# Moving six steps of a scan out of the first norm's chain and into the first tiles of two fused transformer layers

## The reference, cut to what matters

```python
def step(H, inp):
    k_t, v_t, q_t, a_t = inp
    pred = jnp.einsum('bk,bkv->bv', q_t, H)
    err = jnp.sum((v_t - pred) ** 2, axis=-1, keepdims=True)
    surprise = jax.nn.sigmoid(err / (SURPRISE_TEMP + 1e-06))
    kH = jnp.einsum('bk,bkv->bv', k_t, H)
    delta = k_t[:, :, None] * (v_t - kH)[:, None, :]
    a = a_t[:, :, None]
    H = a * H + (1.0 - a) * (surprise[:, :, None] * delta)
    y_t = jnp.einsum('bk,bkv->bv', q_t, H)
    return (H, y_t)
...
x = x + ga * _L0_attn_ref(h, ...)
h = _layernorm(x, axis=-1) * (1 + cb) + sb
x = x + gb * _L0_ffn_ref(h, L0_ffn_w_gate_up, L0_ffn_w_proj)
```

## Time and profile before

| | |
|---|---|
| median of three executions | 1300.75 us |
| the profiled execution | 1301.84 us |
| its span, first to last instruction | 1299.9 us |
| mean granted TensorE clock | 0.880 |
| PE busy over the span | 1135.4 us (87%) |
| DVE busy over the span | 873.2 us (67%) |
| ACT busy over the span | 524.2 us (40%) |
| prefix and its start | 260.90 to 303.64 us |
| tiles 0 to 11 | 303.64 to 433.73 us |

### The profile page before, as it was taken

How to read it: one execution, slowest core, us unless ns; L and a number is a source line. 1 busy time by engine, 2 the same in 40 slices (tenths; PEclk the granted TensorE clock), 3 DMA queues, 4 the chain that set the end, 5 groups by cost and what they waited for, 6 DMA issues and landing times. The chain is left out here.

```text
span 1299.9 us, 13519 instructions
## 1 busy us (share of the span) xinstructions
PE 1135.4 (87%) x4632; PEld 602.2 (46%) x4632; DVE 873.2 (67%) x1602; ACT 524.2 (40%) x1091; POOL 169.7 (13%) x143
## 2 busy tenths in 40 slices
PE   5666879868999779989798988899998999989997
PEld 5423658645656334434344434344443444434443
DVE  3557775554666757879857886768887577883554
ACT  2433554324544236634326425236543163341421
POOL 3000000001111122211112112122301000110100
PEclk9667575556988889989899998999999999999999
DMA  7511111041222013323213001112120001100000
GB/s 219 176 33 33 43 39 49 1 162 49 83 81 81 1 48 113 116 58 111 71 50 95 24 25 57 41 33 87 40 65 9 1 21 63 47 32 1 1 33 32
DMA packets 47525, 75.57 MB, mean 58 GB/s; under 512 B 8321, under 2 KB 16001, under 8 KB 47329
## 3 DMA queue, kind: packets, MB, share of 16 engines
q1 hardware_dynamic: 47168, 74.62, 18.0%
q0 software_dynamic: 288, 0.09, 0.1%
HBM read 66.16 MB, written 8.54 MB: 57 GB/s over the span
## 5 line engine op out<-in xcount | busy, mean ns | idle before, releaser
L1560 PE MATMUL g_g<-h,wt 128*128 128x512 f16 x1728 | 410.6, 387 | 11.7 <-PEq L2440 6.7
L1560 PEld LDWEIGHTS g_g<-h,wt 128*128 128x128 bf16 (+1 forms) x1728 | 170.1, 99 | 236.0 <-issue 50.0
L1574 PE MATMUL g_d<-wt,parts 128*128 128x512 bf16 (+1 forms) x864 | 208.4, 383 | 7.9 <-DVE tmp L1672 3.5
L1483 PE MATMUL g_o<-shared 128*128 128x512 f32 x384 | 182.8, 620 | 16.3 <-ACT hf L2052 9.4
L2144 ACT ACTIVATE parts<-hid 128x512 f16<-128x512 f32 x108 | 68.1, 630 | 318.5 <-DVE hid L1842 313.0
L1835 DVE SCALAR_TENSOR_TENSOR hid<-th,g_g 128x512 f32<-128x512 f32 x108 | 73.6, 682 | 168.8 <-ACT th L2137 168.8
L1574 PEld LDWEIGHTS g_d<-wt,parts 128*128 128x128 f16 x864 | 84.0, 99 | 119.8 <-issue 23.0
L1483 PEld LDWEIGHTS g_o<-shared 128*128 128x128 f32 x384 | 75.2, 199 | 101.0 <-issue 73.9
L2251 POOL TENSOR_TENSOR acc<-acc,sqh 128x512 f32<-128x512 f32 x52 | 77.5, 1489 | 334.1 <-ACT sqh L2150 334.1
L1847 DVE TENSOR_TENSOR parts<-hid,parts 128x512 f16<-128x512 f32 x108 | 82.9, 768 | 31.9 <-ACT parts L2144 31.6
L1492 PE MATMUL g_o<-shared 128*128 128x512 f32 x128 | 64.2, 649 | 10.2 <-DVE shared L1919 5.2
(11 more groups left out here) (312 smaller groups left out, 1649.8 us busy)
## 6 DMA issues: line engine op xcount, KB each, us to landing
shared<-in_w SPq DMA_DIRECT2D x48, 256.0 KB, 2.7
x<-in_codes SPq DMA_DIRECT2D x32, 264.0 KB, 3.1
w_raw<-in_wt SPq DMA_DIRECT2D x16, 512.0 KB, 3.7
x<-in_wmod SPq DMA_DIRECT2D x7, 1024.0 KB, 5.2
wmod<-in_wmod SPq DMA_DIRECT2D x5, 1024.0 KB, 10.7
codes_f<-x SPq DMA_DIRECT2D x32, 132.0 KB, 1.7
gates<-in_x SPq DMA_DIRECT2D x4, 1024.0 KB, 5.8
x<-in_x SPq DMA_DIRECT2D x4, 1024.0 KB, 6.2
```

What stands on the lines that cost most here:

```text
L1483: mm = nc.tensor.matmul(dst[:], w1[:, n % 4, k], xmix[:, w, k], start=(k == 0), stop=(k == KD - 1))
L1560: mm = nc.tensor.matmul(pg[i][:], wide[:, k, o:o + P], h16[f % 2][:, s, k], start=(s == 0 and k == 0), stop=(s == 1 and k == KD - 1))
L1574: mm = nc.tensor.matmul(pd[j][:], parts16[:, t % 3, s, j * P:(j + 1) * P], wd[:, m, :], start=(m == 0 and s == 0), stop=(done and s == 1))
```

## The change

`scan_step` gives no step to a negative q. Tile t (0 to 11) takes steps 2t at q = 3t and 2t + 1 at q = 3t + 1, and none at 3t + 2; the last step is at q = 34 where it was at q = 35. The calls in the three `prefix` functions go. In DVE's `side`, `scan_second(q - 1)` now stands ahead of `scan_first(q)`, since two steps can lie in neighbouring thirds and the second one overwrites what the first one's weighting reads.

```diff
     def scan_step(q):
 
-        n, odd = (q + PREFIX - 1, 0) if q < 0 else divmod(q - 1, 2)
-        n += 0 if q < 0 else PREFIX - 1
-        return (HC + n // (R + 1), n % (R + 1)) if 0 <= n < STEPS and not odd else None
+        tile, third = divmod(q, 3)
+        n = 2 * tile + third
+        return (HC + n // (R + 1), n % (R + 1)) if 0 <= n < STEPS and third < 2 else None
...
         def prefix(q):
-            if scan_step(q):
-                scan_unit(*scan_step(q))
...
         def prefix(q):
-            scan_first(q)
             if q == -7:
                 y_squares(0)
                 first_bounds()
...
             down_steps(q)
-            scan_second(q)
...
                     attention(f, j)
                     norm_stats(f, j)
+            scan_second(q - 1)
             scan_first(q)
-            if q:
-                scan_second(q - 1)
...
         def prefix(q):
-            scan_part(q)
             if q == -6:
                 y_columns(0)
```

## The result

The changed kernel takes 1317.34 us in the median of four executions (1315.38 to 1320.25), against 1300.99 for the kernel before in the same comparison: a ratio of 1.0114, 95% interval 1.0093 to 1.0134. It is slower, by 16.4 us (1.1%); the forecast was 1311 and its range 1299 to 1323.

What follows compares the result with a forecast made beforehand. A dependent chain bounds the prefix, PE bounds tiles 0 to 11. Terms -15.7 + 6.0 + 16.5 + 1.1 - 0.9 (old waits) + 3.2 = +10.2 us on the profiled 1301.84 give 1312.0, so 1311 in the median; range 1299 to 1323.

Steps and rivals of the forecast that it cites:

- The prefix: Stage before tile 0: without scan steps its chain of dependent work ends sooner, -15.7 us (13.5 to 16.5).
- The added work: PE in the tiles: six more scan steps, five of 0.83 us and one of 1.83, +6.0 us.
- The new wait: PE in tiles 0 to 10 idles after the up projection until DVE's `up_product` and weighting: 11 x 1.5 = +16.5 us.
- Tile 11: Second step waits 3.5 us behind DVE's attention row tile, but PE already waited there, so only +1.1 us.
- The clock: Tiles with a section: the gap keeps PE's clock low for one more group of 8 in two of six, +3.2 us.
- The rival of a falling clock: Tiles 0 to 11: clock falls for one group of eight in each, 19 us instead of 3.2; 1327 us, chance 0.12.
- The faster rival: Tiles: weighted rows are ready when the up projection ends, so no gap; -10.6 us, 1290 us, chance 0.12.
- The smaller prefix: Stage before tile 0: something else bounds it and it gives only 8 us; +18, 1319 us, chance 0.06.
- no difference: Prefix gives 15.7 us but the tiles' wait is only 0.9 us each; time stays at 1301 us, chance 0.08.

Runs made afterwards that it cites:

- spaced version: Changed kernel with its 24 scan steps at every other third (q = 1, 3, ..., 47), settled test moved from q = 41 to 49: 1290.8 us.
- Pairs only: Against the kernel before: six steps stay in the prefix, the other 18 go in pairs in thirds 0 and 1 of tiles 0 to 8: 1318.1 us.
- weighting first: Changed kernel with the first step's weighting moved on DVE ahead of `up_product`: 1302.1 us, ratio 0.9997 to the kernel before.

## Why the prediction was right, and which term was off

The direction, the mechanism of the wait and the range held. Of the terms, the clock's was too small, and tile 11's with it.

*The prefix.* Forecast 15.7, measured 15.5; the intermediate instants are within 0.1 us where I give them above.

*The added work.* 6.0 us agrees with the account. The spaced version shows that it need not be paid in full: in tiles 12 to 16 it costs 3.7.

*The new wait.* Forecast twelve waits near 1.5 us, one of them 3.5. The profile shows them, 18.4 us by its count, which starts 0.2 us late in each. The sequence behind it was read rightly in the kernel before, and moving the weighting takes 15 us of the time away, while lengthening the sequence adds to it. One wait was not counted, 0.5 us for the first step of tile 1.

*Tile 11* was mis-sized: forecast +1.1, measured +5.8 (14.3 us from projection to tile 12, against 8.5). I counted the groups behind the 3.6 us wait at the high clock; they ran at the low one, so this is in part the clock's term.

*The clock* is the term that was off: forecast 3.2, measured 14 at most in the profiled execution. I let the low stretch last one group of 8 more in two of the section tiles, and gave tile 11 nothing. The trace after has 13 us more of low clock in tiles 3, 5 and 9 together, 7 us of loss at most, and as much again in tile 11. In tile 5 the clock falls a second time behind the wait (0.93, then 0.60). The place that I named, the gap behind a section's slow projection, was right; how much lies there was not. In the other three executions, whose mean clock of 0.882 or 0.883 means 19 to 22 us less at the low level, the term must have been smaller, but they were also only 1.7 to 4.9 us shorter; between 3 and 12 us is what this leaves for them, by an estimate that puts the whole difference into this stage.

*The rival of a falling clock*, with 19 us and 1327, came nearer with its sum than with its mechanism: it let the clock fall in each of the twelve tiles, and six of them have no fall at all. The measured 1317 lies between it and the forecast. The clock of the stage, 0.83, lies between the 0.87 that I gave for the forecast and the 0.8 that I gave for this rival. The rule that I cited for it (the Trainium skill, TensorE: Matmul & The Clock Gate, A second HAM failure mode: psum-queue depth-cycling), that short repeated idle spells can make the clock swing, agrees with these runs in part: with gaps near 2.6 us the clock falls in five of the six even tiles, with gaps of 1.5 us in none of them.

*The faster rival* would have needed the weighting before the projection's end. The version that does this has no gain either, 1302: its waits are 3.3 us, but its clock stays at 0.84. The wait at which I let the two rivals' sums be zero, 0.9 us a tile, left out my own terms for the clock and for tile 11; with them it is 0.6. *The smaller prefix* is refuted by its 15.5 us, and *no difference* by the waits' length.

In the median the change is 16.4 us where the sum had 10.2. That it stayed within the range has some luck in it: in the profiled execution the clock's excess, up to 11 us, has against it 2.6 us by which the stage before happened to end sooner, and 1.6 us less of waits than I had counted with tile 11.

## What to carry to other kernels

When work leaves an idle stage for one that an engine fills, its cost is first its length and then the distance to the step it depends on: find, on the engine that makes its input, the instruction that stands ahead of it in program order, and what that one waits for. The same 24 steps are worth -10 us or +16 us by where in the tiles they stand. On PE, price a repeated gap at its length first, and then ask whether the clock will follow. Here gaps of 1.5 us in tiles of dense matmuls cost their length and no more; behind a stretch that was already at the low clock, or with 1.1 us more of gap, the clock followed, and a further microsecond of wait cost 2.0 to 2.4.

## What the runs showed of the hardware that was not expected

- Adding 48 matmuls of 128x512 in the gaps, some 10 us of work, did not make the kernel slower but 6 us faster (medians 1317.3 and 1311.5), with the granted clock of the stage at 0.89 in place of 0.83 in the profiled executions.
- Gaps of 1.2 to 1.3 us by the profile left the clock of the six even tiles at 1.00; gaps of 2.4 us brought it to 0.74 to 0.85 in five of them.
- Pairs only scattered widely, from 1306.0 to 1321.1 us in nine executions, the clock with it (0.884 to 0.874); the kernel before went from 1299.6 to 1305.5 in nineteen, weighting first, with 3.3 us of waits, from 1299.1 to 1304.3 in ten.
- A weighting (two instructions of 128x64, float32) took 0.47 us alone, but 1.37 beside a POOL instruction of 128x512 that itself took 1.76, where the mean of its kind is 1.49 before.
